# Attention with paired heads on row halves, three score banks, two double banks of maxima, and the stack transfer issued behind the next group's rows

## The reference

```python
B, N, C = x.shape            # 2, 1024, 288
nh = NUM_HEADS               # 16
hd = C // nh                 # 18
qkv = (h @ w_qkv + b_qkv).reshape(B, N, 3, nh, hd).transpose(2, 0, 3, 1, 4)
q, k, v = (qkv[0], qkv[1], qkv[2])
attn = jax.nn.softmax(jnp.einsum('bhqd,bhkd->bhqk', q, k) * hd ** (-0.5), axis=-1)
o = jnp.einsum('bhqk,bhkd->bhqd', attn, v).transpose(0, 2, 1, 3).reshape(B, N, C)
```

## Time and profile before

| | before |
|---|---|
| median of 3 runs (lowest to highest) | 993.4 us (990.72 to 993.65) |
| profiled execution: its time, its span | 992.99 us, 991.2 us |
| busy: PE, PEld | 900.9 us (91%), 639.9 us (65%) |
| busy: DVE, ACT, POOL | 566.0 us (57%), 516.8 us (52%), 313.3 us (32%) |
| mean granted clock of TensorE | 0.944 |

### The profile page before, as it was taken

One profiled execution on the slowest core, in us unless ns is written; L12 is line 12 of the kernel. 1 busy time (PEld: TensorE's weight loads), 2 busy tenths in 40 slices (PEclk: granted clock), 3 DMA queues, 4 the chain that ended last, 5 costly groups with the idle time before them and its releaser, 6 DMA issues. The chain is left out here.

```text
span 991.2 us, 15201 instructions
## 1 busy us (share of the span) xinstructions
PE 900.9 (91%) x5111; PEld 639.9 (65%) x5111; DVE 566.0 (57%) x978; ACT 516.8 (52%) x1003; POOL 313.3 (32%) x314
## 2 busy tenths in 40 slices
PE   4878799999999999999999896438999999999995
PEld 3775444454545545555444375328999999999995
DVE  3767658767676776767774068463455444444342
ACT  1531266777776777777778735435443333333331
POOL 3522111012120111111042149626555444444342
PEclk9898799999999999999999969558999999999998
DMA  8051600624216060330631157405332222222221
GB/s 209 10 114 23 129 3 17 131 84 102 64 27 137 17 128 19 74 84 8 153 98 44 35 162 256 149 25 141 84 60 56 44 43 43 36 41 40 43 36 19
DMA packets 59296, 73.99 MB, mean 75 GB/s; under 512 B 24856, under 2 KB 51334, under 8 KB 58200
## 3 DMA queue, kind: packets, MB, share of 16 engines
q1 hardware_dynamic: 50216, 60.32, 24.5%
q0 software_dynamic: 8400, 12.12, 7.3%
q10 hardware_dynamic: 608, 0.59, 0.2%
HBM read 33.87 MB, written 15.73 MB: 50 GB/s over the span
## 5 line engine op out<-in xcount | busy, mean ns | idle before, releaser
L1014 DVE TENSOR_REDUCE negmax<-m_ps 128x1 f32<-128x1024 f32 x256 | 309.2, 1221 | 129.5 <-PE m_ps L1079 128.8
L1001 ACT ACTIVATE probs<-s_ps 128x512 f32<-128x512 f32 x486 | 282.0, 597 | 102.6 <-PE s_ps L1110 79.8
L1110 PE MATMUL s_ps<-stack 96*128 96x512 f32 x486 | 212.4, 444 | 5.4 <-ACT probs L1001 3.6
L1110 PEld LDWEIGHTS s_ps<-stack 96*128 96x128 f32 x486 | 90.7, 189 | 163.0 <-ACT probs L1001 130.3
L1079 PE MATMUL m_ps<-stack 96*128 96x512 f32 x512 | 167.7, 412 | 13.1 <-DVE negmax L1014 7.4
L449 POOL TENSOR_TENSOR parts<-proj_f,parts 128x512 fp32r<-128x512 f32 x32 | 41.0, 1282 | 322.0 <-ACT proj_f L443 322.0
L1124 PE MATMUL o_ps<-probs,v_aug 128*19 128x512 f32 x1024 | 136.1, 604 | 0.5 <-ACT probs L1001 0.5
L1969 PE MATMUL gate_bank<-weights,ht_hi 128*128 x630 | 127.1, 296 | 0.4 <-DVE ht_lo L1865 0.4
L1079 PEld LDWEIGHTS m_ps<-stack 96*128 96x128 f32 x512 | 97.9, 195 | 35.2 <-DVE negmax L1014 16.7
L1945 PE MATMUL h_ps<-weights,xt_hi 128*128 x525 | 115.7, 351 | 4.1 <-DVE xt_hi L1858 4.1
L1691 ACT CAST ht_hi<-ht_ps 128x384 fp32r<-128x384 f32 x105 | 43.5, 488 | 117.4 <-PE ht_ps L1956 117.4
(11 more groups left out here) (213 smaller groups left out, 1111.7 us busy)
## 6 DMA issues: line engine op xcount, KB each, us to landing
stack<-parts SPq DMA_DIRECT2D x96, 256.0 KB, 5.0
w_raw<-in_L_cond_w SPq DMA_DIRECT2D x9, 432.0 KB, 3.6
w_raw<-in_L_cond_w SPq DMA_DIRECT2D x9, 384.0 KB, 3.4
xn_scratch<-h SPq DMA_DIRECT2D x16, 192.0 KB, 3.7
x_in<-in_x SPq DMA_DIRECT2D x4, 576.0 KB, 9.6
o_scratch<-o_norm SPq DMA_DIRECT2D x16, 144.0 KB, 2.4
o_in<-o_scratch SPq DMA_DIRECT2D x16, 144.0 KB, 2.6
xr<-in_x SPq DMA_DIRECT2D x16, 144.0 KB, 3.1
```

Source lines behind the costliest of these rows:

```text
L1001: nc.scalar.activation(probs[:, st % 2, h], score_bank(g, st, h), ACT.Exp, scale=SCALE)\
L1014: nc.vector.tensor_reduce(negmax[:, half, g % 2, m % 16:m % 16 + 1], m_ps[m % 2][:], AX.X, ALU.max, negate=True).then_inc(max_free, 1)
L1110: nc.tensor.matmul(score_bank(g, st, h), stack[s][:, h, 1, kt // QT, (kt % QT) * P:(kt % QT + 1) * P], stack[s][:, h, 0, half], start=True ...
```

## The change

- **Row halves.** A stack now has 128 partitions: heads 0 and 2 lie in partitions 0 to 63, heads 1 and 3 in 64 to 127 (`BLOCK` = 64). A head's three products take 3 x 18 = 54 rows, two more hold the maximum, whose counterpart on the keys' side is a row of ones that GpSimd writes once (`ones_rows`). Scores are matmuls of 56 rows, maxima of 54; the two heads of a pair follow each other directly and write into different banks. A tile of maxima (an item) is now 2 blocks, one of each head of a pair, over 512 keys, so that VectorE gives 128x2 maxima of 512 each out of the same 1024 scores, and one more reduction per turn joins the halves (`rowmax`).
- **Banks.** `misc` is gone. Scores and projections share `s_ps`, three banks used in turn (`score_item`, `proj_item`, semaphores `slot_mm`, `slot_free`); rows and outputs take a turn in the two double banks `m_ps`.
- **Order.** `MaxPlan` replaces `plan`: 48 blocks (24 items) ahead of step 0, then 4 blocks a step. A step is now: scores of heads 0 and 1, an item, values, scores of heads 2 and 3, an item or a turn, and in steps 1, 4, 7 and 10 a projection. `four_banks` is gone.
- **Projections.** ScalarE takes a unit out once, and GpSimd makes both the high part (a copy) and the low one. The wait for the stack's transfers moves from ScalarE to GpSimd.
- **Stacks and transfers.** Three stack buffers; transfers of 18 partitions in place of 32; the stack of g+2 is issued in group g behind the rows of the first half of g+1.

```diff
--- before.py
+++ after.py
+    BLOCK = 64
+    MAX_ROW = 3 * HD
+    STACKS = 3
...
-        self.stacks = [sb(stack, "stack0", [3 * HP, GH, 2, 2, HALF], F32R)]
+        self.stacks = [sb(stack, f"stack{i}", [P, 2, 2, 2, HALF], F32R) for i in range(2)]
...
+    def ones_rows(self, pool, i):
+
+        for hh in range(2):
+            s = slice(hh * self.BLOCK + HP, (hh + 1) * self.BLOCK)
+            pool.memset(f32(self.stacks[i][s, :, 1]), 1.0).then_inc(self.ones_ok, 1)
+            pool.wait_ge(self.ones_ok, 2 * i + hh + 1)
...
     def load_stack(self, sp, g):
-        sp.wait_ge(self.parts_ok, 4 * (g + 1))
-
-        n = HP
+        sp.wait_ge(self.parts_ok, self.parts_count(g, 3))
+        sp.wait_ge(self.ones_ok, 2 * min(g + 1, self.STACKS))
         kinds = (slice(self.Q_HI, self.K_HI + 1), slice(self.Q_HI, self.K_LO + 1, 2), slice(self.Q_LO, self.K_HI + 1, 2))
         for h in range(GH):
             for q, kind in enumerate(kinds):
-                sp.dma_start(f32(self.stacks[g % 2][q * HP:q * HP + n, h]).rearrange("p a b n -> p a (b n)"),
-                             f32(self.parts[h * HP:h * HP + n, kind]).rearrange("p a b n -> p a (b n)"))\
+                row = (h % 2) * self.BLOCK + q * HD
+                sp.dma_start(f32(self.stacks[g % self.STACKS][row:row + HD, h // 2]).rearrange("p a b n -> p a (b n)"),
+                             f32(self.parts[h * HP:h * HP + HD, kind]).rearrange("p a b n -> p a (b n)"))\
                   .then_inc(self.stack_ld[h], 16)
...
+S_BANKS = 3
+AHEAD = 48
+RATE = 4
+PROJ_AT = (1, 4, 7, 10)
...
+    def __init__(self):
+        self.lead, self.steps, self.last = [], [[] for _ in range(STEPS * GG)], []
+        self.rows_at, self.out_at, self.count, self.block = {}, {}, 0, 0
+        self.maxima(self.lead, BLOCKS)
+        self.turn(self.lead, "rows", 0)
+        self.maxima(self.lead, AHEAD)
+        due = []
+        for t, items in enumerate(self.steps):
+            g, st = t // STEPS, t % STEPS
+            begun = self.block // BLOCKS
+            self.maxima(items, AHEAD + RATE * t + 2)
+            for turn in due:
+                self.turn(items, "rows", turn)
+            if st == KT + 2:
+                self.turn(items, "out", 2 * g)
+            if st == 2 and g >= 1:
+                self.turn(items, "out", 2 * g - 1)
+            self.maxima(items, AHEAD + RATE * (t + 1))
+            due = range(begun, self.block // BLOCKS)
+        self.turn(self.last, "out", 2 * GG - 1)
...
+            def parts(g, u):
+                half, a = u // 2, u % 2
+                hi, lo = ((heads.Q_HI, heads.Q_LO), (heads.K_HI, heads.K_LO))[a]
+                pool.wait_ge(slot_free, S_BANKS + proj_item(g, u) + 1)
+                if u == 0:
+                    for h in range(GH):
+                        pool.wait_ge(stack_ld[h], 48 * g)
+                nc.gpsimd.tensor_copy(heads.parts[:, hi, half], heads.proj_f[:, u % 2]).then_inc(parts_ok, 1)
+                pool.wait_ge(parts_ok, heads.parts_count(g, u) - 1)
+                nc.gpsimd.tensor_tensor(heads.parts[:, lo, half], heads.proj_f[:, u % 2],
...
-                for kh in range(2):
-                    mm = nc.tensor.matmul(m_ps[m % 2][:, kh * HALF:(kh + 1) * HALF],
-                                          stack[s][:, h, 0, half, qt * P:(qt + 1) * P], stack[s][:, h, 1, kh],
+                for i in range(count):
...
+                    r = slice(hh * heads.BLOCK, hh * heads.BLOCK + heads.MAX_ROW)
+                    mm = nc.tensor.matmul(m_ps[n % 2][:, i], stack[s][r, j, 0, half, qt * P:(qt + 1) * P], stack[s][r, j, 1, kh],
                                           start=True, stop=True)
...
-                    scores(g, st, (0,))
-                    for tile in tiles[:1]:
-                        maximum(*tile)
-                    scores(g, st, (1,))
+                for st in range(STEPS):
+                    items = plan.steps[STEPS * g + st]
+                    scores(g, st, 0)
+                    for it in items[:1]:
+                        item(*it)
                     if st >= 1:
                         values(g, st - 1)
                     elif g >= 1:
                         values(g - 1, STEPS - 1)
-                    scores(g, st, (2,))
-                    for tile in tiles[1:2]:
-                        maximum(*tile)
-                    scores(g, st, (3,))
-                    for tile in tiles[2:]:
-                        maximum(*tile)
-                    for turn in row_turns:
-                        rows(*turn)
-                    for turn in out_turns:
-                        outputs(*turn)
-                    for unit in units:
-                        project(*unit)
+                    scores(g, st, 1)
+                    for it in items[1:2]:
+                        item(*it)
+                    unit = PROJ_AT.index(st) if st in PROJ_AT and g + 2 < GG else None
+                    if unit is not None:
+                        project(g + 2, unit, slice(0, 4))
+                    for it in items[2:]:
+                        item(*it)
+                    if unit is not None:
+                        project(g + 2, unit, slice(4, len(PRODUCTS)))
```

More of the change, by code:

```diff
@@ L568, in _ @@
             nc.gpsimd.memset(f32(wqk_lo[:]), 0.0).then_inc(bias_zero, 1)
+            pool.wait_ge(bias_zero, 4)
+            for i in range(2):
+                heads.ones_rows(pool, i)
             def roots(b):
@@ L968, in _ @@
         def _(act):
[L970 to L981 removed]
+            act.sem_inc(slot_free, S_BANKS)
@@ L982, in _, with out_of_bank @@
+            def out_of_bank(turn):
+                act.wait_ge(pv_free, 2 + KT * (turn + 1))
+                if turn >= 2:
+                    act.wait_ge(max_mm, plan.out_at[turn - 2] + 1)
+                nc.scalar.copy(o_sb[:, turn % 2], o_ps[:]).then_inc(o_evac, 1)
+            for u in range(UNITS):
+                project(1, u)
             for g in range(GG):
                 for st in range(STEPS):
-                    units = plan(g)[1][st - 1] if st >= 1 else []
-                    for unit in units:
-                        heads.high(act, *unit, misc)
@@ L1005, in _ @@
+                    if st in PROJ_AT and g + 2 < GG:
+                        project(g + 2, PROJ_AT.index(st))
+            out_of_bank(2 * GG - 1)
         @block.vector
@@ new lines, in outputs, with item @@
+            def outputs(n, turn):
+                pe.wait_ge(max_free, n + 1)
+                pe.wait_ge(o_evac, turn + 1)
+                for t in range(QT):
+                    mm = nc.tensor.transpose(max_bank(n)[:, t * P:(t + 1) * P], o_sb[:, turn % 2, t * P:(t + 1) * P],
+                                             ident[:])
+                mm.then_inc(max_mm, 1)
+            def item(n, kind, turn, first, count):
+                if kind == "max":
+                    maxima(n, turn, first, count)
+                elif kind == "rows":
+                    rows(n, turn)
+                else:
+                    outputs(n, turn)
@@ new lines, in scores @@
+            def scores(g, st, j):
+                half, kt, s = st // KT, st % KT, g % heads.STACKS
+                if kt == 0:
+                    pe.wait_ge(rows_ld[half], 64 * (g + 1))
+                for hh in range(2):
+                    k = score_item(g, st, 2 * j + hh)
+                    pe.wait_ge(slot_free, k + 1)
+                    r = slice(hh * heads.BLOCK, hh * heads.BLOCK + heads.MAX_ROW + 2)
+                    nc.tensor.matmul(s_ps[k % S_BANKS][:], stack[s][r, j, 1, kt // QT, (kt % QT) * P:(kt % QT + 1) * P],
+                                     stack[s][r, j, 0, half], start=True, stop=True).then_inc(slot_mm, 1)
```

360 lines of the change are left out of this document (158 added, 202 removed).

## The result

The changed kernel takes 947.5 us (median of 4 runs, 946.91 to 948.75) against 993.5 us of the kernel before on the same chip. The profiled execution has a span of 945.1 us.

The account below looks back on a forecast made before the run. A ring of TensorE and ScalarE through two score banks sets the pace. Attention's end at 110.2 + 6 x 52.9 + 49.0 + 45.8 = 522.4 us, now 565.0, is 42.6 us less: 951 us, range 922 to 985.

Parts of the forecast that it names:

- The ring: Attention step before the change: TensorE and ScalarE wait for each other in turn through two score banks, 3.29 us.
- Row pairs at 0.23 us: Two matmuls on different row halves overlap fully and take 0.23 us together; without overlap 0.46 us.
- Plain step: Attention step without projection, values to values: 2.28 + 0.23 + 0.23 + 0.20 = 2.94 us.
- the first rival: The ring through head 3's exponential binds: step 2.67 to 2.83 us, time 920 to 937 us; chance 0.17.
- e2: Head 2's exponential on ScalarE: starts 1.52 us after values, ends at about 2.11; next head 1 needs its bank.
- the chain through e3: Values wait for head 3's exponential (e3), which directly follows head 2's: 1.52 + 1.09 + 0.06 = 2.67 us.
- A projection's step: Attention step with a projection: TensorE sets the pace, 3.91 us, 0.97 us over a step without one.
- Turns: Copies of `o_ps`, and rows and outputs in the maxima's banks: 1.8 us, taken as 2.0 us a group.
- The last group: Its 12 steps without items wait for head 3's exponential, 2.67 us each; the group takes 45.8 us.
- The rival of the clock: TensorE's idle time lowers its clock: slower from 29 of 128 steps, chance 0.09; last group's 12 alone give 969 us.
- The start: Eighteen-row transfers start attention 4.2 us earlier, ones cost 2.8 us; with 2.5 us for half clock, step 0 at 110.2.
- GpSimd waits instead: In group 0 GpSimd takes ScalarE's 4.5 us wait for transfers; the stack transfer is hidden, first needed 20 us later.

## Why the prediction was right, and where it was not

**The ring.** The reading that TensorE and ScalarE alternate through the score banks held: giving back the row halves costs 74 us (19 of them by the clock), giving back the third bank 75 us.

**Row pairs at 0.23 us.** Right: side by side on opposite halves two take what one takes (0.23 us less per pair than on the same half). No sign of the estimated 0.30 us: the chain from head 1 to values is 0.66 us, the 0.23 + 0.23 + 0.20 of the sum.

**Plain step.** 2.83, not 2.94 us. The 0.11 us between the load of head 1's weights and its matmul, taken over from the earlier trace rows, did not appear: both have 399.30 us. The 0.20 us for the change of form was right in size. So the step lies at the edge of what the first rival forecast (2.67 to 2.83), but not by its mechanism: head 1 does wait for e2's bank, and the change costs 0.20, not 0.09. With the items moved out of the way, the steps of 2.66 us show the chain through e3 that this rival had.

**A projection's step.** The term that was sized too small is the two switches around the products. The step was predicted at 3.91 us and measured at 4.13 without a turn. TensorE in step 1 of group 5:

```profile
379.48 1.05 PE L1179 MATMUL o_ps<-probs,v_aug 128*19 128x512 f32 x8 [0.34 <-ACT o_sb L1040]
380.46 0.50 PE L1165 MATMUL s_ps<-stack 56*128 56x512 f32 x2
...
381.12 0.97 PE L441 MATMUL s_ps<-stretch,wqk_hi 128*128 128x512 f32 x3
...
382.95 0.50 PE L1165 MATMUL s_ps<-stack 56*128 56x512 f32 x2
...
383.62 1.05 PE L1179 MATMUL o_ps<-probs,v_aug 128*19 128x512 f32 x8
```

Pair and item take 0.66 us for 0.46 us of streaming, the seven products 1.83 us for 1.61. So each of the two passages between the row halves and the 128-row products costs 0.2 us, as much as the one to the values, where I had put down 0.2 us for both: 0.42 - 0.2 is the 0.22 us that were missing. With a turn the step takes 4.53 and 4.91 us, since an item then stands between the fourth product and the fifth and makes two passages more. Weight loads of TensorE around those, in step 4 of group 5:

```profile
392.74 0.19 PEld L441 LDWEIGHTS s_ps<-stretch,wqk_lo 128*128 128x128 f32 x1 [0.24 <-issue]
...
393.64 0.19 PEld L1165 LDWEIGHTS s_ps<-stack 56*128 56x128 f32 x2 [0.36 <-issue]
```

In these gaps the trace shows nothing that is waited for. By the rule of the Trainium skill ("TensorEngine Tiling (Array Packing)", "Key Properties") a change of tiling mode drains TensorE; the 0.2 us per passage agrees with it.

**Turns.** 2.5 us a group in place of 2.0: the two copies' steps are 3.23 us (predicted 3.26), 0.4 us each over a plain one, step 2 has 0.5 us, and steps 4 and 10 the 0.4 and 0.8 us named above. A group is 9 x 2.83 + 17.7 + 2 x 3.23 + 3.34 = 53.0 us, predicted 52.9. The agreement is luck: the plain step was 16 x 0.11 = 1.8 us too long, the projections (1.30 us over a plain step, predicted 0.97) 4 x 0.33 = 1.3 us and the turns 0.5 us too short, and these cancel.

**The last group.** 2.66 us a step, predicted 2.67. The first of these steps from values to values, and the last values of attention:

```profile
489.43 1.05 PE L1179 MATMUL o_ps<-probs,v_aug 128*19 128x512 f32 x8
492.09 1.05 PE L1179 MATMUL o_ps<-probs,v_aug 128*19 128x512 f32 x8
...
522.38 1.06 PE L1179 MATMUL o_ps<-probs,v_aug 128*19 128x512 f32 x4 [1.17 <-ACT probs L1033]
```

The rival of the clock was real in its mild form: the profiled execution kept 0.99, others of nearly the same program lost it, at 11 us.

**The start.** The transfers of 18 partitions were not shorter than those of 32: 13.63 us for twelve against 13.72, so the 4.2 us were false, and the prediction had named the condition. SP's queue, and GpSimd and TensorE in the lead-in:

```profile
58.51 13.63 SPq L473 DMA_DIRECT2D stack<-parts  x12
...
72.90 3.65 POOL L434 MEMSET stack<- 32x2048 f32 x2 [14.41 <-POOLq L485]
...
79.12 1.65 PE L441 MATMUL s_ps<-stretch,wqk_hi 128*128 128x512 f32 x3 [2.97 <-POOL wqk_hi L402]
```

The price of the ones, 2.8 us, was right (2.97 us of wait). The first item comes at 73.24 us and not at 70.5. Step 0 starts at 110.9 us, where 110.2 had been put down, and that it is so near is luck again: the 2.5 us held back for the half clock in group 0 came in small part only (group 0 took 53.05 us from values to values and a later group 53.0, of which 0.5 us are a turn in step 2 that group 0 has not), and they stand in for the 3 us by which the block began too late.

**GpSimd waits instead.** Right in the sum and wrong in its reason. I had the stack's transfer as hidden by the distance to its first use and the wait as one of group 0; in fact it reaches into every next group, and the move of the wait is worth 50 us. The theory I wrote before the run on this repeated the mistake.

**Behind attention.** The last values come at 522.38 us, forecast 522.4, 42.6 us before the old place. The nearness is chance as well: step 0 was 0.7 us late, the six groups 0.5 and the last group 0.5 us longer, group 6 with 47.25 in place of 49.0 us shorter by their sum. The other 3.5 us of the gain lie after them, where nothing was changed: 945.1 - 522.4 = 422.7 us in place of 991.2 - 565.0 = 426.2. A window 10 us after the last values, before and after:

```profile
575.00:585.00 10.00, 10.00 (x37) 7.88 (x35) 4.77 (x14) 1.95 (x6) 2.45 (x4) 0.50 0.34 97
```

```profile
532.40:542.40 10.00, 10.00 (x54) 8.16 (x54) 6.67 (x20) 3.25 (x11) 3.98 (x5) 0.84 0.61 175
```

TensorE is back at 2.4 GHz sooner here. Over the twelve experiments this stretch took from 420.0 to 426.7 us with the same code, so the 3.5 us are within what it varies by; why is open.

## What to carry to other kernels

Where two engines hand banks to each other, write the ring out as start times and ask of each edit which edge it shortens; here neither the pairs on row halves nor the third bank shortened a group without the other, and the whole change took 5.9 us off it. When a step becomes shorter, add up the other engines over the whole round: with VectorE at 2.44 of 2.66 us, and 0.2 us of TensorE for every change of form, five orders of the same items ended within 1.4 us of a 53 us group. And when a transfer is issued later, look for whoever waits for it, and let an engine with nobody behind it do so.

## What the hardware showed unexpectedly

- Work of no use can pay for itself: with four unused 54-row matmuls in each thin step the granted clock was 1.00 where it had been 0.50, and the median 8.4 us lower.
- The same edit of GpSimd's order, which took 3 us out of the lead-in, was followed some 420 us later by a fall of the clock that put the last values 11 us back. Whether the edit caused the fall isn't shown; a difference of this size in the median need not lie where the edit is.
- A transfer from SBUF to SBUF keeps SP's queue 1.1 us, whether of 32 or of 18 partitions (13.72 and 13.63 us for twelve), and ScalarE's 1.3 us (7.88 us for six).
- Each change between matmuls on a row half and the 128-row products, either way, and from them to the values, took TensorE some 0.2 us (0.66 - 0.46, 1.83 - 1.61 and 0.66 - 0.46 us).
- A matmul on one row half runs beside one on the other even if they belong to different lines of work: in plain steps an item between the scores of a pair cost nothing (2.66 us either way).
